# Attention row sums in a fused attention and feed-forward block: 16 of 72 probability tiles per group summed by accumulating transfers, ring of 21 tiles

## What is computed

```python
q = (x @ wq).reshape(b, s, NH, HD)
k = (x @ wk).reshape(b, s, NKV, HD)
v = (x @ wv).reshape(b, s, NKV, HD)
k = jnp.repeat(k, NREP, axis=2)
v = jnp.repeat(v, NREP, axis=2)
scores = jnp.einsum('bihd,bjhd->bhij', q, k) * SCALE
scores = jnp.where(causal, scores, jnp.finfo(scores.dtype).min)
attn = jax.nn.softmax(scores, axis=-1)
out = jnp.einsum('bhij,bjhd->bihd', attn, v)
return out.reshape(b, s, NH * HD) @ wo
```

## Time and profile before

| | us |
|---|---|
| median of 3 runs | 3474.51 |
| lowest and highest run | 3471.63, 3475.09 |
| the profiled execution, its own time | 3474.3 |
| span of its core | 3472.5 |
| PE busy | 3410.8 (98%) |
| VectorE busy | 2008.2 (58%) |
| ACT busy | 1459.9 (42%) |
| POOL busy | 1746.1 (50%) |

### The profile page before, as it was taken

How to read it: one execution, slowest core, us unless ns; L and a number is a source line. 1 busy time by engine, 2 the same in 40 slices (tenths; PEclk the granted TensorE clock), 3 DMA queues, 4 the chain that set the end, 5 groups by cost and what they waited for, 6 DMA issues and landing times.

```text
span 3472.5 us, 61790 instructions
## 1 busy us (share of the span) xinstructions
PE 3410.8 (98%) x25202; PEld 2398.6 (69%) x25202; DVE 2008.2 (58%) x3617; ACT 1459.9 (42%) x1830; POOL 1746.1 (50%) x749
## 2 busy tenths in 40 slices
PE   8999999999999999999999999999999999999998
PEld 7888886566666666666666666666658888878887
DVE  3122117777677677677777767767756666642222
ACT  3111113555555555555555555555543333211111
POOL 0000003888988898898898898889550000000000
PEclk9999999999999999999999999999999999999999
DMA  6334343021112112111112111110037777655553
GB/s 216 112 124 124 115 137 93 24 53 50 35 43 50 38 38 52 49 30 48 50 33 53 50 35 43 50 38 11 26 101 234 231 236 233 220 204 170 170 175 131
DMA packets 248556, 340.60 MB, mean 98 GB/s; under 512 B 55648, under 2 KB 150368, under 8 KB 248288
## 3 DMA queue, kind: packets, MB, share of 16 engines
q1 hardware_dynamic: 248288, 336.87, 32.5%
HBM read 203.08 MB, written 133.17 MB: 97 GB/s over the span
## 4 chain that ended last, share of the span: by engine, by line
PE 95%; DVE 2%; ACT 2%; issue 0%; DMA 0%; ACTq 0%; SPq 0%; DVEq 0%
PE p_o L758 19%; PE p_qm L709 16%; PE p_acc L42 13%; PE p_acc L44 12%; PE p_acc L43 12%; PE p_km L751 12%; PE p_km L744 3%; PE p_qm L713 2%; DVE p_part_max L870 2%; PE p_km L746 2%; ACT p_probs L834 2%; PE p_ag_ps L1185 1%; PE p_acc L1174 1%; PE p_ag_ps L1186 1%; PE p_sm_ps L1200 0%
## 5 line engine op out<-in xcount | busy, mean ns | idle before, releaser
L870 DVE TENSOR_REDUCE p_part_max<-p_qm 128x1 f32<-128x512 f32 (+3 forms) x2240 | 1406.9, 671 | 568.4 <-PE p_qm L709 326.5
L681 POOL TENSOR_TENSOR p_psums<-p_psums,p_probs 128x1024 f32<-128x1024 f32 x620 | 1478.4, 2385 | 91.9 <-ACT p_probs L834 2.5
L834 ACT ACTIVATE p_probs<-p_km 128x1024 f32<-128x1024 f32 x896 | 878.4, 1021 | 481.1 <-PE p_km L751 442.5
L709 PE MATMUL p_qm<-p_k_st,p_q_st 96*128 96x512 f32 (+3 forms) x2560 | 904.3, 415 | 3.3 <-DVE p_part_max L870 1.3
L709 PEld LDWEIGHTS p_qm<-p_k_st,p_q_st 96*128 96x128 f32 x2560 | 473.9, 191 | 243.9 <-issue 102.1
L751 PE MATMUL p_km<-p_q_st,p_k_st 97*128 97x512 f32 x1792 | 598.8, 416 | 15.7 <-ACT p_probs L834 9.6
L758 PE MATMUL p_o<-p_probs,p_v 128*32 128x256 f32 (+1 forms) x9216 | 565.7, 372 | 0.0
L758 PEld LDWEIGHTS p_o<-p_probs,p_v 128*32 128x32 f32 x9216 | 270.9, 110 | 217.0 <-issue 45.1
L751 PEld LDWEIGHTS p_km<-p_q_st,p_k_st 97*128 97x128 f32 x1792 | 311.6, 191 | 116.1 <-ACT p_probs L834 73.5
L677 POOL TENSOR_TENSOR p_psums<-p_probs 128x1024 f32<-128x1024 f32 x110 | 261.8, 2380 | 202.5 <-ACT p_probs L834 202.5
L666 POOL MEMSET p_k_st<- 1x2048 f32 x2 | 3.6, 1804 | 511.4 <-PE p_acc L44 511.4
(11 more groups left out here) (153 smaller groups left out, 3988.3 us busy)
## 6 DMA issues: line engine op xcount, KB each, us to landing
p_q_st<-q_hi SPq DMA_DIRECT2D x128, 256.0 KB, 4.6
p_x_raw<-in_xT SPq DMA_DIRECT2D x64, 256.0 KB, 3.5
q_hi<-p_out_hi SPq DMA_DIRECT2D x64, 256.0 KB, 2.0
q_lo<-p_out_lo SPq DMA_DIRECT2D x64, 256.0 KB, 2.4
p_q_st<-q_lo SPq DMA_DIRECT2D x64, 256.0 KB, 4.3
attended_T<-p_o_raw SPq DMA_DIRECT2D x128, 128.0 KB
p_a_raw<-attended_T SPq DMA_DIRECT2D x32, 512.0 KB, 10.1
p_recip<-reciprocals SPq DMA_DIRECT2D x128, 128.0 KB, 7.0
```

The source lines that it names most:

```text
L681: pool.tensor_tensor(sums[:, :, :], sums[:, :, :], probs[(n * NS + s) % PB][:, :, :], ALU.add).then_inc(added, 1)
L709: last = pe.matmul(bank[:, x * keys:(x + 1) * keys], q_st[par][0:ROWS, c, h + x, sub * P:(sub + 1) * P], k_st[par][0:ROWS, j * CK:j * CK + ...
L834: act.activation(tile[:, :, :].rearrange("p h q -> p (h q)"), km[s % 2][:, :, :].rearrange("p a b -> p (a b)"), ACT.Exp, scale=SCALE).then ...
L870: dve.reduce_max(part_max[c][:, h:h + heads, sub, j], qm[bank_of(i)][:, 0:item_width(i)].rearrange("p (h k) -> p h k", h=heads), AX.X).the ...
```

## The change

The ring `probs` has 21 tiles in place of 22, and the space goes to one new tile `fsums`. In each of the first 15 groups the sums of chunks 3 to 7 are split in three:

- The first 2, 3, 3, 4 and 4 tiles of the chunk ("fetched") are summed in `fsums` by transfers. SP copies tile 0 into it, SBUF to SBUF, and POOL's queue issues one accumulating transfer (`accum_op=ALU.add`) for each of tiles 1, 2 and so on. Each waits for the one before it to land.
- The next 4, 6, 7, 8 and 10 tiles are added in `psums` by POOL instructions as before. One more such instruction (L748 of the new program), just ahead of the chunk's last add, takes `fsums` into `psums` once all transfers have landed.
- PE makes passes of ones over what is left.

Chunks 0, 1 and 2 and the last group keep their plans. ACT, before it reuses a ring tile, waits for the copy or the transfer that read it.

```diff
-    PB = 22
+    PB = 21
...
-    POOLED = [0, 3, 5, 6, 8, 9, 11, 12]
-    SUMS = Sums(POOLED)
-    LAST_SUMS = Sums([c + 1 if c > 2 else 0 for c in range(NC)])
...
+    def order(fetched, added):
+
+        if not added:
+            return []
+        tiles = list(range(fetched, fetched + added))
+        steps = [("copy", 0)] if fetched else []
+        steps += [("first", tiles[0])]
+        fetches = [("fetch", t) for t in range(1, fetched)]
+        for x, t in enumerate(tiles[1:]):
+            steps.append(("add", t))
+            if x % 2 == 0 and fetches:
+                steps.append(fetches.pop(0))
+        assert not fetches
+        if fetched:
+            steps.insert(len(steps) - 1, ("fetched", 0))
+        return steps
+
+    SUMS = Sums([order(*counts) for counts in ((0, 0), (0, 3), (0, 5), (2, 4), (3, 6), (3, 7), (4, 8), (4, 10))])
+    LAST_SUMS = Sums([order(0, c + 1 if c > 2 else 0) for c in range(NC)])
...
+        fsums = sb("p2_fsums", [P, REP, CQ], F32)
...
+            def begin_fetched(n, c):
+
+                earlier = [e for e in range(c) if SUMS.copied_before[e + 1] > SUMS.copied_before[e]]
+                if earlier:
+                    sp.wait_ge(added, n * NADD + SUMS.adds_through_fetched(earlier[-1]))
+                elif n > 0:
+                    sp.wait_ge(added, (n - 1) * NADD + SUMS.adds_through_fetched(NC - 1))
+                sp.wait_ge(exp_done, n * NS + FIRST_STEP[c] + 1)
+                sp.dma_start(fsums[:, :, :], probs[(n * NS + FIRST_STEP[c]) % PB][:, :, :]).then_inc(copied, 16)
...
+                            events.append((FIRST_STEP[c] + 3.6, "begin fetched", c))
...
+                        elif what == "fetch":
+                            pool.wait_ge(exp_done, n * NS + s + 1)
+                            pool.wait_ge(copied, 16 * copies)
+                            at_least(pool, fetched, 16 * landed)
+                            pool.dma_start(fsums[:, :, :], tile[:, :, :], accum_op=ALU.add).then_inc(fetched, 16)
+                            landed += 1
+                        elif what == "fetched":
+                            pool.wait_ge(fetched, 16 * landed)
+                            pool.wait_ge(added, adds)
+                            pool.tensor_tensor(sums[:, :, :], sums[:, :, :], fsums[:, :, :], ALU.add).then_inc(added, 1)
+                            adds += 1
+                        elif first is not None:
+                            pool.wait_ge(exp_done, n * NS + s + 1)
                             at_least(pool, chunk_done, n * NCHUNK + max(0, plan.chunks[c] - 1))
-                            pool.tensor_tensor(sums[:, :, :], probs[(n * NS + s - 1) % PB][:, :, :], probs[(n * NS + s) % PB][:, :, :],
-                                               ALU.add).then_inc(added, 1)
+                            pool.tensor_tensor(sums[:, :, :], first[:, :, :], tile[:, :, :], ALU.add).then_inc(added, 1)
+                            first = None
+                            adds += 1
...
-                    if not plan.on_pool(s):
+                    if plan.on_pe(s):
                         last = weighted(ones[:, :], probs[(n * NS + s) % PB], CQ, offset(s), False)
```

More of the change, by code:

```diff
@@ L391, in attend, with __init__ @@
     class Sums:
[L393 to L398, removed]
+        def __init__(self, orders):
+            self.orders = orders
+            counted = lambda kinds: [sum(what in kinds for order in orders[:c] for what, _ in order) for c in range(NC + 1)]
+            self.adds_before, self.copied_before, self.fetched_before = (
+                counted(("add", "fetched")), counted(("copy",)), counted(("fetch",)))
+            self.chunks = [sum(bool(order) for order in orders[:c]) for c in range(NC + 1)]
@@ L399, in on_pool, with on_pe, first_pair @@
+        def on_pe(self, s):
             c, t = STEPS[s]
-            return t < self.pooled[c]
+            return (t not in self.first_pair(c) and ("add", t) not in self.orders[c]
+                    and not any(what in ("copy", "fetch") and tile == t for what, tile in self.orders[c]))
+        def first_pair(self, c):
+            return [tile for what, tile in self.orders[c] if what == "first"]
         def adds_through(self, s):
             c, t = STEPS[s]
-            return self.adds_before[c] + max(1, t)
@@ L406, in attend, with fetched_through @@
-    POOLED = [0, 3, 5, 6, 8, 9, 11, 12]
-    SUMS = Sums(POOLED)
-    LAST_SUMS = Sums([c + 1 if c > 2 else 0 for c in range(NC)])
-    NADD, NCHUNK = SUMS.adds_before[NC], SUMS.chunks[NC]
+            at = self.orders[c].index(("first", t) if t in self.first_pair(c) else ("add", t))
+            return self.adds_before[c] + max(1, sum(what in ("add", "fetched") for what, _ in self.orders[c][:at + 1]))
+        def fetched_through(self, s):
+            c, t = STEPS[s]
+            order = [tile for what, tile in self.orders[c] if what == "fetch"]
+            return self.fetched_before[c] + order.index(t) + 1 if t in order else 0
@@ new lines, in copied_through, with adds_through_fetched @@
+        def copied_through(self, s):
+            c, t = STEPS[s]
+            return self.copied_before[c] + 1 if ("copy", t) in self.orders[c] else 0
+        def adds_through_fetched(self, c):
+            return self.adds_before[c] + 1 + sum(
+                what == "add" for what, _ in self.orders[c][:self.orders[c].index(("fetched", 0))])
+    def order(fetched, added):
[13 more added lines that the diff above has]
+        return steps
@@ L504, in attend @@
         added = sem("p2_added")
+        copied = sem("p2_copied")
+        fetched = sem("p2_fetched")
         chunk_done = sem("p2_chunk_done")
@@ L587, in group @@
                     events.append((s + 1.3, "next max" if ahead else "max", c))
+                if not last:
+                    for c in range(NC):
+                        if SUMS.copied_before[c + 1] > SUMS.copied_before[c]:
+                            events.append((FIRST_STEP[c] + 3.6, "begin fetched", c))
                 if started:
@@ L612, in group @@
                         opening.load_next_rows(sp)
+                    elif what == "begin fetched":
+                        begin_fetched(n, c)
                     elif what == "load q":
@@ L671, in group @@
                     sums = psums[c % 2]
-                    for t in range(1, plan.pooled[c]):
+                    adds, landed = n * NADD + plan.adds_before[c], n * NFETCH + plan.fetched_before[c]
+                    copies = n * NCOPY + plan.copied_before[c]
+                    for what, t in plan.orders[c]:
                         s = FIRST_STEP[c] + t
-                        pool.wait_ge(exp_done, n * NS + s + 1)
-                        if t == 1:
+                        tile = probs[(n * NS + s) % PB]
+                        if what == "copy":
+                            copies += 1
+                        elif what == "first":
+                            first = tile
+                        elif what == "fetch":
[11 more added lines that the diff above has]
+                            pool.wait_ge(exp_done, n * NS + s + 1)
@@ L684, in gpsimd @@
+                            first = None
+                            adds += 1
+                        else:
+                            pool.wait_ge(exp_done, n * NS + s + 1)
+                            pool.wait_ge(added, adds)
+                            pool.tensor_tensor(sums[:, :, :], sums[:, :, :], tile[:, :, :], ALU.add).then_inc(added, 1)
+                            adds += 1
             group(0, SUMS)
@@ L804, in output @@
             def output(n, c, plan):
-                if plan.pooled[c]:
+                if plan.orders[c]:
                     act.wait_ge(chunk_done, n * NCHUNK + plan.chunks[c + 1])
@@ L822, in exps @@
                 at_least(act, slot_done, (n if u >= 0 else n - 1) * NSL + SLOT_OF[u % NS] + 1)
-                if plan.on_pool(u % NS):
+                if plan.copied_through(u % NS):
+                    at_least(act, copied, 16 * ((n if u >= 0 else n - 1) * NCOPY + plan.copied_through(u % NS)))
+                elif plan.fetched_through(u % NS):
+                    at_least(act, fetched, 16 * ((n if u >= 0 else n - 1) * NFETCH + plan.fetched_through(u % NS)))
+                elif not plan.on_pe(u % NS):
                     at_least(act, added, (n if u >= 0 else n - 1) * NADD + plan.adds_through(u % NS))
```

7 lines of the change are left out of this document (3 added, 4 removed).

## The result

The change makes the kernel slower: median 3756.9 us in 4 runs (3747.1 to 3770.5) against 3473.1 us in 4 runs of the kernel before, a ratio of 1.082 with a 95% interval of 1.0807 to 1.0833. The forecast was 3756 us.

A forecast was written before the change was run, and what follows sets the result against it. PE was taken to set the pace, with POOL 1.0 us ahead in chunk 7. 14 steady groups of 14.1 us net plus 5.1 of low clock, and 13 for the opening group, add 282 to 3474.3: 3756 us, range 3600 to 4000.

The forecast's parts named there:

- part 4: POOL starts chunks later, so PE waits 3.2, 5.6 and 7.5 us ending chunks 4, 6, 7; steady group 14.1 us longer.
- the 5 to 8 us that were named as the sign: Sign of being right: PE waits 5 to 8 us for POOL's L759 at its `psums` pass in chunks 6 and 7.
- The gain: Five full PE passes of ones fewer in a group, 0.43 us each: 2.15 us a group, 32 us over 15 groups.
- part 2: POOL's load: 47 instructions a group become 41, plus 11 transfer issues of 1.0 us each; 114 us in some 125.
- part 3: Time for an accumulating transfer of 512 KB to land: 5.5 us, range 3.5 to 8.
- part 5: PE's lower clock behind each of the three waits costs 1.7 us, 5.1 us a group, between nothing and twice that.
- The opening group: The first group, with longer steps from more row-maximum items, was counted as 13 us longer.
- What I cost at nothing: SP's five copies a group and the ring's one tile less were taken to add no time.
- The cheap case: Rival: issue 0.44 us, landing 3.5; waits 1.2, 2.5 and 5.8 us, 10.7 us a group with the clock, 3631 us; chance 0.19.
- The slow chain: Rival: landing 8 us, each transfer waits for the one before, all four chunks make PE wait; 4055 us; chance 0.18.
- POOL keeping up: Rival: POOL in time in chunk 7, ten instructions in 20.6 us, saved passes show in full: 3442 us; chance 0.03.

The follow-up runs named there:

- the spread order: Changed kernel, same tile counts, but POOL starts with tiles 1 and 2 and transfers take tile 0 and later spread tiles: 3489.0 us, ratio 1.004 to the kernel before.
- the filled kernel: Changed kernel with 4, 9 and 13 additional PE passes of ones ahead of the waits ending chunks 4, 6 and 7: 3645.0 us, ratio 1.050 to the kernel before.
- the order with six passes saved: The spread order with 60 tiles a group off PE in place of 59 and fsums taken up last or last but one: 3445.1 us, ratio 0.9909 to the kernel before.

## Why the prediction was right

**The mechanism, point by point.** The step that carried the forecast was part 4: POOL's first instruction of a chunk has to wait for a later tile, and the sum then misses PE's fixed place. It holds. Chunks 4, 6 and 7 wait and chunks 3 and 5 do not, as worked out, though chunk 6's waits, 2.4 to 5.4 us and all but one under 5, stay below the 5 to 8 us that were named as the sign; the spread order, with all the transfers in place, takes nearly all of the loss away.

**The gain** of five passes of 0.43 us a group is there: with the order mended and POOL in time, six passes gave 29 of 38 us.

**The issue** (part 2) was taken at 1.0 us and is 0.74. **The landing** (part 3) was taken at 5.5 us and is 4.6; the range of 3.5 to 8 held both the median and nearly the maximum of 8.9. With these two values the same steps give waits of 2.3, 4.2 and 6.7 us, 13.2 a group, where I had 3.2, 5.6 and 7.5, together 16.3. Measured are 178.4 us in 15 groups, 9.7 of them in the opening one, so 12.0 in a steady group. Of the last 1.2 us, up to 1.0 go with the low clock: in the filled kernel, where the clock stays up, POOL is up to 13.0 us late. I put this down to the low clock slowing PE on its way to the pass, so that POOL has more time; that the filling does nothing else to POOL was not tried by itself.

**The low clock** (part 5) is the term that was mis-sized. I took 1.7 us behind each of three waits, 5.1 a group. A group grew by 145.7 - 125.5 = 20.2 us; less 12.0 of waits, plus 2.15 of saved passes, 10.3 us are left for it. PE's own busy time says the same: 1847.15 / 14 = 131.9 us a group against 1732.47 / 14 = 123.7, 8.2 more with 2.15 less to do. The filled kernel gave 8.5 of it back, although POOL was up to 1.0 us later there. I had read one pause of 2.2 us, with 3.4 us at the lower level behind it, and carried that over to all three waits. The stretches were longer here, and not only behind the longer waits: in this execution eight of the twelve waits of 1.9 us were followed by 10.2 us at the lower level, and four by none. Four us too much in waits and five too little in clock cancelled to within 1 us a group. Over the fourteen groups that is 60 us too much and 75 too little. The opening group grew by 13 us, as forecast (296 us in all, less 283 in the fourteen). So the profiled execution came out 14 us above the forecast, and the median of the four lies another 14 us below it: that it meets 3756 to 1 us is luck.

**What I cost at nothing**, the ring, costs nothing. SP's copies did hold up something once they had to be early: in the order with six passes saved.

**The rivals.** The cheap case (3631 us) had issue and landing too low and counted the clock at a third of what it cost. The slow chain did not come: two adds and an issue, 5.76 us, cover a landing of 4.6, and the few transfers that took longer, as in the group shown, held POOL for under 10 us in the whole run. POOL keeping up was excluded by ten instructions in 20.6 us, and so it was.

## What to carry to other kernels

An engine that is busy 73% of the time (1492.35 of 2040.3 us; it was 89% before) can be late three times in every group, if its work starts later: look at when the first operand of each sum is there and when the sum is wanted, not at the load. When part of a chain of adds is handed to something slower to land, hand over tiles from its middle and leave the adding engine the first ones. And a wait of the matrix engine can cost more than its length, because of the clock behind it: here 12.0 us of waits in a group brought 10.3 us of slower work.

## What the runs showed of the hardware

- Behind a wait of PE the granted clock can fall to the lower of its two levels (1.2 GHz in place of 2.4), and how long it stays there does not follow from the wait alone. In the group shown, 1.90 us of waiting left it at 1.00, behind 4.45 us it was 0.77 over 15 us, and around 6.95 us 0.54 over 15 us. Two groups earlier, 1.93 us were followed by 10 us at the lower level:

```profile
1352.70 0.64 PE L836 MATMUL p_o<-p_psums,p_ones 128*32 128x256 f32 x8 [1.93 <-POOL p_psums L759]
```
```profile
1353.50:1363.50 10.00, 8.87 (x32) 6.19 (x35) 4.33 (x8) 4.87 (x6) 7.17 (x4) 0.50 0.33 68
```

In the kernel without accumulating transfers the wait at the end of chunk 7 is 4.3 us in each of the fourteen steady groups, and the stretch at the lower level is now 10.2, now 13.7, now 6.8 us long. Three groups in a row:

```profile
835.00:855.00 20.00, 17.10 (x125) 10.06 (x126) 9.25 (x15) 8.44 (x11) 10.54 (x6) 0.74 0.27 66
968.00:988.00 20.00, 17.21 (x110) 9.74 (x114) 8.89 (x14) 7.84 (x10) 9.01 (x5) 0.66 0.19 53
1104.00:1124.00 20.00, 18.64 (x138) 10.97 (x142) 11.49 (x19) 10.74 (x14) 11.49 (x6) 0.83 0.28 74
```

- An accumulating transfer of 512 KB within SBUF, issued by POOL, lands after 4.6 us (4.5 to 8.9) and a plain one after 2.9 (2.9 to 5.9). The issue is in the profile with 869 and 567 ns; by spacing the first keeps POOL 0.74 us.
- POOL's adds did not slow down beside these transfers: the take-up and the last add of chunk 7 start 2.48 us apart, against 2.51 in the earlier trace rows, with the DMA engines busy 0.39 of the time in place of 0.17. Only the add right behind an issue is longer, and that is within the 0.74 us.
